# The second pass of a graph-attention block masked by GpSimd and VectorE instead of TensorE and VectorE, with its loop written out

## The reference

```python
# x: (16, 512, 512) f32, adj: (16, 512, 512) int32, 16 heads of 32
h = jnp.maximum(_layernorm(x, axis=-1), 0.0)
q = heads(h @ Wq + bq); k = heads(h @ Wk + bk); v = heads(h @ Wv + bv)
scores = jnp.einsum('bhqd,bhkd->bhqk', q, k) * scale
scores = jnp.where(adj[:, None] == 0, -jnp.inf, scores)
attn = jax.nn.softmax(scores, axis=-1)
out = jnp.einsum('bhqk,bhkd->bhqd', attn, v)          # heads side by side again
return x + out @ Wo + bo
```

## Time and profile before

| | us |
|---|---|
| median of three runs | 1778.74 (1775.16 to 1779.21) |
| span of the profiled execution, first to last instruction | 1774.9 |
| TensorE busy | 1702.4 (96%) |
| VectorE busy | 1450.9 (82%) |
| ScalarE busy | 1447.0 (82%) |
| GpSimd busy | 140.8 (8%) |
| one block, in blocks outside the loop | 105.9 |

### The profile page before, as it was taken

How to read it: one execution, slowest core, us unless ns; L and a number is a source line. 1 busy time by engine, 2 the same in 40 slices (tenths; PEclk the granted TensorE clock), 3 DMA queues, 4 the chain that set the end, 5 groups by cost and what they waited for, 6 DMA issues and landing times.

```text
span 1774.9 us, 32235 instructions
## 1 busy us (share of the span) xinstructions
PE 1702.4 (96%) x8129; PEld 1040.2 (59%) x8256; DVE 1450.9 (82%) x3493; ACT 1447.0 (82%) x3397; POOL 140.8 (8%) x200
## 2 busy tenths in 40 slices
PE   3889999999999999999999999999999999999997
PEld 2646666665666556665666656656566665666643
DVE  5778888888888888888888888888888888888783
ACT  2688888887888888888888878888788888888884
POOL 0000100000000011100000000001100001010010
PEclk9999999999999999999999999999999999999999
DMA  5434333333434334343333433334333333433311
GB/s 166 112 85 109 97 103 86 111 89 105 109 92 111 82 113 109 96 102 83 111 91 105 110 90 108 88 113 107 99 98 86 113 91 107 110 95 96 84 61 36
DMA packets 118720, 175.64 MB, mean 99 GB/s; under 512 B 32385, under 2 KB 34433, under 8 KB 118529
## 3 DMA queue, kind: packets, MB, share of 16 engines
q1 hardware_dynamic: 114432, 172.35, 36.0%
q10 hardware_dynamic: 4096, 1.06, 0.3%
HBM read 54.79 MB, written 16.78 MB: 40 GB/s over the span
## 4 chain that ended last, share of the span: by engine, by line
PE 88%; DVE 4%; ACT 2%; issue 2%; SPq 2%; DMA 1%; POOL 0%; ACTq 0%; DVEq 0%; POOLq 0%
PE ps L723 16%; PE psO L754 14%; PE psP L647 14%; PE ps L734 13%; PE psP L649 12%; PE psP L648 12%; PE ps L737 5%; PE ps L695 2%; ACT ps L397 1%; DVE x_tile L468 1%; PE ps L701 1%; DVE ps L544 1%; SPq L270 1%; SPq L266 1%; SPq L273 1%
## 5 line engine op out<-in xcount | busy, mean ns | idle before, releaser
L544 DVE CUSTOM_DVE_ANT_0 ps<-ps,bias_q 128x512 f32<-128x512 f32 x1024 | 710.9, 696 | 243.9 <-PE ps L723 229.3
L397 ACT ACTIVATE ps<-ps,neg_max 128x512 f32<-128x512 f32 x1024 | 681.8, 666 | 125.8 <-DVE neg_max L544 85.4
L427 ACT ACTIVATE probs<-ps 128x512 f32<-128x512 f32 x1024 | 614.8, 601 | 88.9 <-PE ps L734 78.8
L723 PE MATMUL ps<-k_stack,q_stack 96*128 96x512 f32 x1024 | 449.7, 439 | 20.4 <-ACT ps L397 11.4
L734 PE MATMUL ps<-q_stack,k_stack 98*128 98x512 f32 x1024 | 409.8, 401 | 4.0 <-ACT probs L427 3.3
L551 DVE SCALAR_TENSOR_TENSOR probs<-bias_k,probs 128x512 f32<-128x512 bf16 x512 | 363.3, 710 | 12.7 <-ACT probs L427 12.7
L723 PEld LDWEIGHTS ps<-k_stack,q_stack 96*128 96x128 f32 x1024 | 192.8, 188 | 270.1 <-ACT ps L397 132.3
L754 PE MATMUL psO<-probs,v_sb 128*32 128x512 f32 x2048 | 274.4, 608 | 2.7 <-DVE probs L551 1.5
L734 PEld LDWEIGHTS ps<-q_stack,k_stack 98*128 98x128 f32 x1024 | 195.1, 191 | 44.0 <-ACT probs L427 17.1
L397 ACT ACTIVATION_READ_ACCUMULATOR ps<-ps,neg_max 128x1 f32 x1024 | 209.0, 204 | 0.0
L737 PE MATMUL ps<-bias_k,ident_b 128*128 128x512 bf16 x385 | 151.1, 392 | 0.0
(11 more groups left out here) (63 smaller groups left out, 1989.8 us busy)
## 6 DMA issues: line engine op xcount, KB each, us to landing
q_stack<-part_hi SPq DMA_DIRECT2D x512, 64.0 KB, 2.0
k_stack<-part_hi SPq DMA_DIRECT2D x512, 64.0 KB, 2.0
x_tile<-in_x_dram SPq DMA_DIRECT2D x64, 256.0 KB, 2.8
adj_tile<-in_adj_dram SPq DMA_DIRECT2D x64, 256.0 KB, 2.9
q_stack<-part_lo SPq DMA_DIRECT2D x256, 64.0 KB, 2.0
k_stack<-part_lo SPq DMA_DIRECT2D x256, 64.0 KB, 2.0
y_tile<-in_x_dram SPq DMA_DIRECT2D x64, 256.0 KB, 2.7
out_dram<-y_tile SPq DMA_DIRECT2D x64, 256.0 KB, 2.1
```

The source lines that it names most:

```text
L397: nc.scalar.activation(item, item, ACT.Exp, scale=-1.0, bias=neg_max[:, g % 2, col:col + 1], accum_out=exp_sum[:, g % 2, col:col + 1]).the ...
L427: nc.scalar.activation(probs[:, n % P_RING, :], ps2[:, n % 2, :], ACT.Exp, scale=SCALE).then_inc(exp2_done, 1)
L544: nc.vector.tensor_tensor_reduce(bank1(("s", u)), bank1(("s", u)), bias_q[:, qt, :], -SCALE, 3.0e38, ALU.add, ALU.min, neg_max[:, g % 2, c ...
L723: nc.tensor.matmul(bank1(("s", u)), q_stack[0:STACK, g, j, P * qt:P * qt + P], k_stack[0:STACK, g, j, :], start=True, stop=True).then_inc( ...
```

## The change

The mask matmuls of pass 2 are dropped. Even items are masked after the exp by GpSimd, with a product of the exp's bits, read as int32, by a tile `keep_k` of ones and zeros. Odd items stay on VectorE, as a minimum of `probs` and `keep_k` times 2^100. `keep_k` is int32 (before, `bias_k` was bf16). To pay for its room, adj tiles are loaded into the two x buffers instead of a buffer of their own, so x tiles 0 and 1 of the next batch are loaded later, at slots 34 and 38 instead of 12 and 15. PV stands one slot later (u % 4 == 3), the last split of `psO` moves into the next block, and the loop of blocks is written out, so that all waits are constants.

```diff
-ADJ_AT = (17, 24, 30, 36)
-BIAS_AT = (24, 30, 36, 46)
+ADJ_AT = (14, 16, 25, 31)
+BIAS_AT = (24, 28, 32, 37)
-VECTOR_MASKED = (1, 3, 5, 7)
-O_HI_AT = {16: 0, 31: 1, 47: 2, 63: 3}
-O_LO_AT = {17: 0, 32: 1, 48: 2, 63: 3}
+O_HI_AT = {1: (3, -2), 16: (0, -1), 32: (1, -1), 48: (2, -1)}
+O_LO_AT = {2: (3, -2), 17: (0, -1), 33: (1, -1), 49: (2, -1)}
...
-        bias_k = sb("bias_k", [P, NT, S], BF16)
+        keep_k = sb("keep_k", [P, NT, S], I32)
...
 # SP
+                    if t >= 2:
+                        sp.wait_ge(h_turned, due(4 * b + t - 1))
+                    else:
+                        sp.wait_ge(bias_done, due(4 * (b - 1) + t + 3))
...
-                    sp.wait_ge(bias_done, due(4 * b + t))
+                    if t < 2:
+                        sp.wait_ge(h_turned, due(4 * b + t + 3))
+                    else:
+                        sp.wait_ge(bias_done, due(4 * b + t - 1))
+                    sp.dma_start(adj_view(t), adj_rows[bass.ds(row, 1)].rearrange("a p d -> (a p) d")
...
-                    if u == 12: load_x(k + 1, 0)
-                    if u == 15: load_x(k + 1, 1)
+                    if u == 34: load_x(k + 1, 0)
+                    if u == 38: load_x(k + 1, 1)
 # GpSimd
+            def mask(b, n):
+                if n == 0:
+                    pool.wait_ge(m_done, due(2 * b + 1))
+                if n == 8:
+                    pool.wait_ge(m_done, due(2 * b + 2))
+                pool.wait_ge(exp2_done, due(64 * b + n + 1))
+                tile = probs[:, n % P_RING, :].bitcast(I32)
+                nc.gpsimd.tensor_tensor(tile, tile, keep_k[:, n % 16 // 4, :], ALU.mult).then_inc(even_masked, 1)
...
+                    if u == 5: form_rstd(k, 2)
+                    if u == 9: add_bo(k - 2, 2)
+                    if u == 10: form_rstd(k, 3)
+                    if u == 13: add_bo(k - 2, 3)
+                    if u == 41: form_rstd(k + 1, 0)
+                    if u == 43: form_rstd(k + 1, 1)
...
+                    b, n = pass2(k, u)
+                    if have(b) and n % 2 == 0:
+                        mask(b, n)
 # VectorE
-                    nc.vector.tensor_copy(bias_k[:, 2 * n:2 * n + 2, :], bank1((kind, n, rel)).bitcast(BF16).rearrange("p (t q) -> p t q", q=S)
-                                          ).then_inc(m_done, 1)
+                    nc.vector.tensor_scalar(keep_k[:, 2 * n:2 * n + 2, :],
+                                            bank1((kind, n, rel)).bitcast(BF16).rearrange("p (t q) -> p t q", q=S),
+                                            0.0, None, ALU.is_equal).then_inc(m_done, 1)
...
-                    if have(b) and n % 8 in VECTOR_MASKED:
+                    if have(b) and n % 2 == 1:
...
-                        nc.vector.scalar_tensor_tensor(out=probs[:, n % P_RING, :], in0=bias_k[:, n % 16 // 4, :], scalar=-MASKED,
-                                                       in1=probs[:, n % P_RING, :], op0=ALU.add, op1=ALU.min
-                                                       ).then_inc(probs_masked, 1)
+                        nc.vector.scalar_tensor_tensor(out=probs[:, n % P_RING, :], in0=keep_k[:, n % 16 // 4, :], scalar=-MASKED,
+                                                       in1=probs[:, n % P_RING, :], op0=ALU.mult, op1=ALU.min
+                                                       ).then_inc(odd_masked, 1)
 # TensorE
+                if T == 0 and kt == NT - 1:
+                    pe.wait_ge(o_hi_done, due(4 * b + 4))
+                    pe.wait_ge(o_lo_done, due(4 * b + 4))
...
-                        if n % 8 not in VECTOR_MASKED:
-                            last = nc.tensor.matmul(ps2[:, n % 2, :], ident_b[:], bias_k[:, kt, :], start=False, stop=True)
-                        last.then_inc(scores2, 1)
...
-                    if u % 4 == 2 and have(k - 1):
+                    if u % 4 == 3 and have(k - 1):
...
-                        pe.wait_ge(exp2_done, due(64 * b + 4 * n + 4))
-                        pe.wait_ge(probs_masked, due(MASKED_ALL * b + masked_before(4 * n + 4)))
+                        pe.wait_ge(even_masked, due(32 * b + 2 * n + 2))
+                        pe.wait_ge(odd_masked, due(32 * b + 2 * n + 2))
```

More of the change, by code:

```diff
@@ L196, in pass2, with adj_view, blocks @@
             return (k, u - S2_AT) if u >= S2_AT else (k - 1, u + SLOTS - S2_AT)
-        def masked_before(n):
-            return n // 8 * len(VECTOR_MASKED) + sum(i < n % 8 for i in VECTOR_MASKED)
-        MASKED_ALL = masked_before(SLOTS)
-        def blocks(eng, block, first=-1, counters=()):
-            for k in range(first, LOOP_FROM):
-                block(k, k % 2)
-            for counter, value in counters:
-                counter.start(value)
-            with eng.Fori(LOOP_FROM, LOOP_TO, 2) as k:
-                block(k, 0)
-                block(k + 1, 1)
-            for k in range(LOOP_TO, B + 2):
-                block(k, k % 2)
+        def adj_view(t):
+            return x_tile[:, t % 2, :].bitcast(I32)
+        def blocks(step, first=-1):
+            for k in range(first, B + 2):
+                step(k, k % 2)
         block = ctx.enter_context(nc.Block())
@@ L261, in load_stack @@
                 sp.wait_ge(scores2, due(64 * (b - 1) + 16 * (g + 1)))
-                sp.wait_ge(qk_hi_done, due(8 * b + i + 1) if known(b) else next_part.reg)
+                sp.wait_ge(qk_hi_done, due(8 * b + i + 1))
                 hi_rows = [r for r in (0, 32, 64) if r != lo_row]
@@ L267, in load_stack @@
                                  part_hi[32 * j:32 * j + 32, i % 2, :].bitcast(F32)).then_inc(stack_in[kind], 16)
-                sp.wait_ge(qk_lo_done, due(8 * b + i + 1) if known(b) else next_part.reg)
+                sp.wait_ge(qk_lo_done, due(8 * b + i + 1))
                 for j in range(GROUP):
@@ L459, in ln_stats @@
                     dve.wait_ge(norm_done, due(4 * b + t - 1))
-                    dve.wait_ge(stats_done, due(4 * b + t + 1) if known(b) else next_stats.reg)
-                    if not known(b):
-                        next_stats.advance()
+                    dve.wait_ge(stats_done, due(4 * b + t + 1))
                     nc.vector.bn_aggr(mean_var[:, t % 2, :], stats[:]).then_inc(aggr_done, 1)
@@ L540, in step @@
                             dve.wait_ge(bias_done, due(4 * b + qt + 1))
-                        dve.wait_ge(scores1, due(64 * b + n + 1) if known(b) else next_scores.reg)
-                        if not known(b):
-                            next_scores.advance()
+                        dve.wait_ge(scores1, due(64 * b + n + 1))
                         nc.vector.tensor_tensor_reduce(bank1(("s", u)), bank1(("s", u)), bias_q[:, qt, :], -SCALE, 3.0e38,
@@ L560, in step @@
                             take_turn(k, kind, n, rel)
-                    if u in O_LO_AT and have(k - 1):
-                        g = O_LO_AT[u]
-                        dve.wait_ge(o_hi_done, due(4 * (k - 1) + g + 1))
+                    g, rel = O_LO_AT.get(u, (0, -B))
+                    if u in O_LO_AT and have(k + rel):
+                        dve.wait_ge(o_hi_done, due(4 * (k + rel) + g + 1))
                         nc.vector.scalar_tensor_tensor(out=oT_lo[:, g, :], in0=psO[:], scalar=bv_col[:, g:g + 1],
```

139 lines of the change are left out of this document (51 added, 88 removed).

## The result

| | before | changed |
|---|---|---|
| median of the runs | 1778.04 us (1775.16 to 1779.21, 4 runs) | 1931.53 us (1926.32 to 1935.91, 4 runs) |
| ratio | 1 | 1.0854, 95% [1.0828, 1.0880] |
| span profiled, mean granted clock | 1774.9 us, 0.995 | 1933.8 us, 0.930 |
| matmuls of TensorE in the trace | 8129 (of the 512 mask matmuls 127 have no record) | 7744 |

The change costs 153 us. The prediction said 1739 us, faster with a chance of 0.82; it has the wrong sign, and the time lies outside its range. One edit of the change stood in no term of it: the first transpose of the mask (`("m", 0, 0)` in `TURNS`) moves from turn 53 to 55, where it stands right ahead of the transpose `("c", 0, 0)` of turn 56.

The account below looks back on a forecast made before the run. TensorE was taken as the bound. From 1774.9 us: minus 118 (mask matmuls), minus 10 (loop), plus 15 (normalise of x tile 3 held by the port), 18 (psO split), 55 (late tile) gave 1735, median 1739; range 1678 to 1782.

Parts of the forecast that it names:

- The mask matmuls and the loop: On TensorE, 512 mask matmuls of 0.23 us removed, 118 us; loop written out, 10 us less (bounds 0 and 12).
- The product: GpSimd's 512 integer products of 128x512: 1.3 to 1.6 us each taken, bounds 1.29 and 2.7; GpSimd not full.
- The lead of VectorE's masks: VectorE's odd-item mask begins some 0.15 us before GpSimd's product, losing the SBUF port only in 4 to 8 of 32.
- The late tile: x tile 1, loaded behind SP's stacks, keeps VectorE waiting about 4.5 us at slot 42; 55 us in all, bounds 0 and 72.
- the forecast's own signs of being wrong: Profile signs named beforehand: long products, most masks over 1.2 us, or no wait for x_tile.
- so pass 1 of slot 46 comes at 9.7 and not 5.9: 3.7 us lost per block: TensorE's stop behind the late x tile, after its three banks run out: 15 times, 55 us.
- Clock 1.00: TensorE's granted clock in a block of the kernel before, taken as full, 2.4 GHz.
- I price it at 0 beside its waits: Masks held by GpSimd at the shared SBUF port: 4 to 8 us of VectorE per block, absorbed by its room.
- the split of the last psO: Moved into the next block, it makes TensorE wait 1.5 us instead of 0.3 before slot 3's projection: 18 us.
- rival (b): The port makes VectorE lose most meetings and become full: slower than before, about 1915 us with 24 lost; 6%.
- rival c: GpSimd's integer product takes over 3.1 us and GpSimd is the bound: near 2000 us at 3.5; 6%.
- rival a: The late x tile costs nothing or little, VectorE being late itself: 1684 us, or 1665 without two smaller waits; 17%.

Follow-up runs that it names:

- e3: The kernel before with its loop of blocks written out and nothing else; 1766.32 us, ratio to before 0.9937.
- e2: The changed kernel with GpSimd's product on one column instead of 512, so even items stay unmasked; 1846.26 us.
- e1: The changed kernel with VectorE's statistics of x tile 1 at slot 47 instead of 42, factor and normalise later too; 1836.19 us.
- e9: The changed kernel with the load of x tile 1 at turn 37 instead of 38, ahead of the stack transfers; 1831.75 us.
- e12: The kernel before, loop written out (e3), with the load of x tile 1 moved from turn 15 to 38; 1834.83 us.
- e10: The changed kernel with the first transpose of the mask at turn 53 again instead of 55; 1880.92 us.
- e5: e1 with the first transpose of the mask back at turn 53 instead of 55; 1787.06 us.
- e4: e1 with GpSimd's product on one column, as in e2 (even items unmasked); 1746.71 us.
- e7: e5 with GpSimd's product on one column (even items unmasked); 1704.73 us.
- e8: The changed kernel with PV one slot earlier again (u % 4 == 2) and the four oT pieces at their old slots; 1885.58 us.
- e6: e5 with PV at u % 4 == 2 and the oT pieces at their old slots, every mask made; 1732.07 us.

## Why the prediction was wrong, step by step

**Right.** The bound: TensorE, fed by three banks. The mask matmuls and the loop: e3 has 11.2 of the loop's 10. The product: 1.41 us in the mean, in the bounds of 1.29 and 2.7, and near the value taken. The lead of VectorE's masks: a twentieth is held, fewer than the 4 to 8 of 32 that the step allowed. The late tile: 4.60 us of wait where 4.5 was worked out, and 5.63 - 1.17 = 4.5 us lost at slot 45 where it was 3.7 (from its own figures, 9.7 - 5.9, it is 3.8); without the product, in e2, it is 4.98 - 1.17 = 3.8, so the rest is the port's. None of the forecast's own signs of being wrong appeared: the products are short, few masks are over 1.2 us, the wait for x_tile is there. The signs watched the steps that had a term; most of the cost came from what had none or was put at nothing.

**Wrong: the clock has no term.** The step "so pass 1 of slot 46 comes at 9.7 and not 5.9: 3.7 us lost per block" ends where TensorE starts again. Its next 6.8 us ran at 0.51. In slots 46 and 47 that is (2.94 - 1.17) + (3.57 - 2.26) = 3.1 us a block more, 0.27 of it a wait. By e1 and e9 the late tile costs 95 to 100 us, not 55; e12 shows the fall without product, shared buffers or the stops at slots 55 and 56. The Trainium skill has the mechanism (TensorE: Matmul & The Clock Gate, section HAM oscillation — how this bites in real kernels): where TensorE starves inside a kernel its clock drops and each burst behind it starts slow. This trace agrees in both places of the block, behind 3.83 us and behind 0.93 and 1.58. "Clock 1.00" was read off the blocks of before, where the longest stop has a median of 0.7 us, and it was kept for a kernel with stops of 4.3. At such stops the lower clock has to be added.

**Wrong: a move without a term.** The transpose of m from turn 53 to 55 was not named. By itself it costs 51 us (e10), 49 on top of e1 (e5), with two banks of three taken in a row and 1.22 us of `keep_k` in front of the next pass 1. `keep_k` itself was priced at "1 us" a block as VectorE's load; as a hold on a bank it is in TensorE's way.

**Wrong: "I price it at 0 beside its waits".** The port costs 85 us (e2), 90 (e4 against e1), 82 (e7 against e5). The rule behind it was used, but on two kinds of instruction only, the masks and the normalise of tile 3. The Trainium skill (SBUF — State Buffer, section Who interferes with whom) names which instructions it can strike: VectorE instructions with two SBUF inputs, beside a GpSimd instruction that reads SBUF, and one-input forms that run in a mode with both ports. The rows agree, and they show that the size doesn't matter: `c_parts` of 16 columns is held for 1.0 us as a mask of 512 is, and `bias_q` takes 0.68 us in the mean and 0.42 in e2. As a share of its length a short instruction loses most. The other half of the step, that room on VectorE absorbs it, fails too: 93.7 us of VectorE in a block of 116.1 is room on average, and none in the slots where it is late, since only three banks stand between it and TensorE.

**Mis-sized: the split of the last psO.** 18 us was the term; slot 3 loses 2.88 - 1.27 = 1.6 us about as worked out, but the edit that brought it costs 46 (e8) to 55 us (e6). The difference is slots that the term didn't look at and, by the half clock of the inner blocks, the clock again. PV and the oT pieces were not tried apart.

Taken as gaps between price and term, the four are 45 for the tile (100 - 55), 70 for the port (85 - 15), 51 for m and 28 for PV and the split (46 - 18): 194 us, against 1931.5 - 1739 = 192.5. Measured on top of one another (e1, e7 against e5, e5, e6) they are 40, 67, 49 and 37, 193 us. Both sums close, so no fifth cause of their size is left; a fit to 2 us is luck, with medians that are good to some 5 us each. The rival (b), "the port decides", was right on the sign and wrong on the way: it had masks lose most meetings and VectorE full, and VectorE never was. In no run was GpSimd the bound (rival c), and the tile did cost (rival a).
